# Set-up weights in later buffers; expert routing done by groups inside the layer loop, its last entries written at the start of the expert block

## The reference, cut to what matters

```python
logits = x_flat @ router_w.T
probs = jax.nn.softmax(logits, axis=-1)
top_v, top_i = jax.lax.top_k(probs, K)                  # K = 2
top_v = top_v / jnp.sum(top_v, axis=-1, keepdims=True)
for k in range(K):
    pos = (rank of the token among those whose k-th choice is this expert)
    keep = pos < C                                      # C = 1280
    h = jax.nn.gelu(jnp.einsum('ech,ehf->ecf', expert_in, w1), approximate=False)
    y = jnp.einsum('ecf,efh->ech', h, w2)
    out = out + tok * (gate * keep)[:, None]
```

## Time and profile before

| | us |
|---|---|
| median of 3 runs | 1517.16 (1514.6 to 1522.25) |
| the profiled execution, its own time | 1516.38 |
| its span, first to last instruction | 1514.6 |
| stack phase, last logits copied at | 932.1 |
| first products of an expert block at | 986.2 |
| last products end at | 1504.2 |

### The profile page before, as it was taken

How to read it: one execution, slowest core, us unless ns; L and a number is a source line. 1 busy time by engine, 2 the same in 40 slices (tenths; PEclk the granted TensorE clock), 3 DMA queues, 4 the chain that set the end, 5 groups by cost and what they waited for, 6 DMA issues and landing times. The chain is left out here.

```text
span 1514.6 us, 51179 instructions
## 1 busy us (share of the span) xinstructions
PE 1386.4 (92%) x19679; PEld 1179.2 (78%) x19680; DVE 852.4 (56%) x2933; ACT 829.0 (55%) x2393; POOL 626.2 (41%) x1265
## 2 busy tenths in 40 slices
PE   4879999999999999999999985299999999999997
PEld 3557777777777777777777763199999999999996
DVE  3578888888888888888888864811111111111110
ACT  0378898988888898988888871111111111111110
POOL 0132434343343424343343320046555555555554
PEclk6799999999999999999999996589999999999999
DMA  9423343434343433434342003446655665566653
GB/s 300 139 68 93 106 118 92 117 96 127 93 131 93 115 110 100 116 94 122 93 118 72 13 13 133 168 149 189 183 173 176 187 186 178 173 182 192 181 174 80
DMA packets 94784, 198.57 MB, mean 131 GB/s; under 512 B 14561, under 2 KB 49058, under 8 KB 84482
## 3 DMA queue, kind: packets, MB, share of 16 engines
q1 hardware_dynamic: 75698, 173.97, 37.1%
q0 software_dynamic: 15904, 18.66, 5.8%
q10 hardware_dynamic: 2992, 3.28, 0.6%
HBM read 177.88 MB, written 17.99 MB: 129 GB/s over the span
## 5 line engine op out<-in xcount | busy, mean ns | idle before, releaser
L1678 ACT ACTIVATE heT<-ps 128x512 f32<-128x512 f32 x142 | 84.8, 597 | 434.9 <-PE ps L1644 434.9
L1644 PEld LDWEIGHTS ps<-xeT,w_block 128*128 128x128 f32 x2272 | 267.5, 194 | 5.2 <-DVE xeT L1575 0.9
L1644 PE MATMUL ps<-xeT,w_block 128*128 128x128 f32 x2272 | 268.2, 277 | 1.0 <-DVE xeT L1555 0.5
L833 ACT ACTIVATE x_prob<-ps,x_nmax 128x257 f32<-128x257 f32 x512 | 237.4, 476 | 47.6 <-DVE x_rinv L1210 38.4
L1630 PE MATMUL ps<-w,heT 128*128 x1136 | 256.8, 379 | 0.0
L1630 PEld LDWEIGHTS ps<-w,heT 128*128 128x128 f32 x1136 | 210.5, 190 | 25.6
L1206 DVE TENSOR_REDUCE x_nmax<-ps 128x2 f32<-128x514 f32 x256 | 167.0, 684 | 19.9 <-PE ps L595 13.2
L1692 POOL TENSOR_TENSOR rt_hold<-constants 128x1 f32<-128x1 f32 x213 | 82.5, 387 | 219.3 <-DMA out<-ye,to_ix 134.0
L603 PE MATMUL ps<-constants,x_prob 128*128 128x128 f32 x1024 | 148.7, 277 | 20.4 <-ACT x_prob L833 19.8
L921 POOL TENSOR_TENSOR query_var_eps<-query_moments,epsilon 128x1 f32<-128x1 f32 x32 | 6.1, 190 | 370.3 <-DVE query_moments L1075 370.3
L837 ACT ACTIVATE x_probT<-ps 128x512 f32<-128x512 f32 x256 | 140.4, 600 | 25.3 <-PE ps L603 24.8
(11 more groups left out here) (283 smaller groups left out, 2841.0 us busy)
## 6 DMA issues: line engine op xcount, KB each, us to landing
w_block<-in_m_w SPq DMA_DIRECT2D x71, 1024.0 KB, 5.1
context<-in_cT SPq DMA_DIRECT2D x128, 257.0 KB, 3.1
context<-in_cn SPq DMA_DIRECT2D x128, 256.0 KB, 4.2
w<-in_m_w SPq DMA_DIRECT2D x8, 1024.0 KB, 12.0
xin<-in_x SPq DMA_DIRECT2D x32, 128.0 KB, 3.0
lastq<-in_lastq SPq DMA_DIRECT2D x32, 128.0 KB, 3.0
context<-in_lastk SPq DMA_DIRECT2D x32, 128.0 KB, 3.8
out<-x SPq DMA_DIRECT2D x32, 128.0 KB, 1.7
```

The source lines that it names most:

```text
L833: A(p1[u % 2][:, r, :], ps[:, r, 0:KEYS], ACT.Exp, bias=nmax1[u % 2][:, r:r + 1], accum_out=rsum1[u % 2][:, r:r + 1]).then_inc(e1_ok.handl ...
L1644: t = mm(ps[:, 2 * b + n, f * P:(f + 1) * P], w1[b][:, k, lo:lo + P], xeT[b][:, k, :], start=k == 0, stop=k == H - 1)
L1678: A(heT[b][:, n * FK // 2:(n + 1) * FK // 2, :].rearrange("p k t -> p (k t)"), ps[:, 2 * b + n, :], ACT.Gelu).then_inc(heT_ok.handle, 1)
```

## The change

**Set-up weights** move to buffers of the stack phase that are used later (`fw_raw` in the probabilities of the 16-head attention, `setup_w` in `query_blocks`, `x5`, `x5_norm`, `outT`). The waits of SP for the end of set-up are gone; each first context is loaded with 3 DMAs in place of 9, and x of tiles 1 to 3 comes right behind context 0.

**Experts' weights** `w2` now share the memory of the ring of contexts: two experts are loaded when one of the last four tiles is done with its context.

**Routing** is done by groups of four tiles in the loop (groups of two for the last four tiles). Per group DVE has 15 `CHOICE` instructions in one slot (the first and second expert, running counts) and 16 `PLACE` instructions in the next (gate, position, address), ACT one exponential, PE two small matmuls (`counted`). Each token's entry (its number and its gate) is written by an indirect DMA of POOL to a table in DRAM, 128 entries per DMA, two DMAs per tile. Tiles 0 to 27 are written in the loop and behind it; tiles 28 to 31 (8 DMAs) at the start of the expert phase. The table of blocks (`block_table`) is computed in between the last `PLACE` steps. Then SP loads the whole table into `places`; a block's rows are one column of it, whose number DVE loads into a register. The gather of gates is gone.

**The order** of the steps in `slot` is new on all engines, as are the banks `B`; s now ends at 35.

```diff
-AHEAD, BEHIND = 6, 3
+AHEAD, BEHIND = 6, 4
+GROUP = 4
+ROUTED_BEHIND = 3
...
-    fw_raw = [context[2][:, n * H * FF:(n + 1) * H * FF] for n in (0, 1)]
+    fw_raw = [p1_both[:].rearrange("p q r k -> p (q r k)")[:, 0:H * FF], p1T_both[:].rearrange("p q r k t -> p (q r k t)")]
...
             load_x(0, 0)
...
-            for b in range(NB):
-                load_batch(0, 0, b)
+            load_context(0, 0)
+            for t in range(1, RING):
+                load_x(t, t)
...
             for t in range(1, RING):
-                load_x(t, t)
-            for b in range(NB):
-                load_batch(1, 1, b)
-            sp.wait_ge(su_cp, SU_CP)
-            sp.wait_ge(su_q, SU_Q)
-            for t in range(2, RING):
-                for b in range(NB):
-                    load_batch(t, t, b)
+                load_context(t, t)
...
+            def write_entry(t, k):
...
+                nc.gpsimd.indirect_dma_start(table, bass.IndirectOffsetOnAxis(ap=place[:, t, k:k + 1], axis=0), entries[:, t, k, :], None).then_inc(table_in, 16)
...
+            CHOICE = [(route_best, route_shifted), (route_first_key, route_first_top), (route_first_hot, route_rest), (route_second, route_second_key),
+                      (route_second_rank, route_second_top), (route_second_hot, route_run(0)), (route_run(1), route_run(2)), (route_run(3),)]
+            PLACE = [(route_sum, route_share), (route_second_share,), (route_where, route_carry), (route_held, route_kept),
+                     (route_gate, route_both), (route_both_columns, route_address), (route_address_sum, route_whole), (route_column, route_column_f, route_place)]
...
+            last = len(GROUPS) - 1
+            for steps in CHOICE:
+                for step in steps:
+                    step(last, *GROUPS[last])
+            table_steps = block_table()
+            for steps in PLACE:
+                for step in steps:
+                    step(last, *GROUPS[last])
+                    next(table_steps, None)
...
+            for t in range(tiles - 4, tiles):
+                for k in range(TOPK):
+                    g.indirect_dma_start(table, bass.IndirectOffsetOnAxis(ap=place[:, t, k:k + 1], axis=0), entries[:, t, k, :], None).then_inc(table_in, 16)
...
+                if first:
+                    sp.wait_ge(table_in, TOPK * tiles * 16)
+                    sp.dma_start(places[:], table.rearrange("(p c) w -> p c w", c=ROW)[:, 0:EXP * tiles + 1, :]).then_inc(places_in, 16)
```

More of the change, by code:

```diff
@@ L124, with stack_phase @@
 RING = 4
-AHEAD, BEHIND = 6, 3
-def stack_phase(nc, t_in, const, logits, ps, constants, consts_loaded, zero, gates, xnorm, out, tiles, sem, sig, sb):
+CONTEXT = NB * KT * D + H * NB * KEYS + NB * OWN
+ROW = 512
+AHEAD, BEHIND = 6, 4
+GROUP = 4
+ROUTED_BEHIND = 3
+def stack_phase(nc, t_in, const, logits, ps, constants, consts_loaded, zero, contexts, w2, w2_in, table, table_in, tab_i, place, entries,
+                xnorm, out, tiles, cap, sem, sig, sb):
     ident = const["ident"]
@@ new lines, in stack_phase @@
+    blocks_i = sb("rt_blocks_i", [P, EXP], I32)
+    tab = sb("rt_tab", [P, 2])
+    GROUPS = [(t, GROUP) for t in range(0, tiles - GROUP, GROUP)] + [(tiles - 4, 2), (tiles - 2, 2)]
+    routed = Steps(sem("routing_step"), ["best", "shifted", "first_key", "first_top", "first_hot", "rest", "second", "second_key", "second_rank", "second_top", "second_hot",
+                                        "sum", "share", "second_share", "where", "held", "kept", "gate", "both", "both_columns", "address", "address_sum",
+                                        "whole", "column", "column_f", "place"])
@@ new lines, in stack_phase, with group_at, tiles_scattered @@
+    tab_ps, tab_ok = sem("block_table_in_psum"), sem("block_table_ready")
+    def group_at(s, half):
+        for g, (first, n) in enumerate(GROUPS[:-1]):
+            if first + n + ROUTED_BEHIND + half == s:
+                return g
+    def tiles_scattered(s):
+        for g, (first, n) in enumerate(GROUPS[:-2]):
+            done = first + n + ROUTED_BEHIND + 2
+            for i in range(n):
+                if s == done + (i if g < len(GROUPS) - 3 else i // 2):
+                    yield first + i
@@ new lines, in _, with routing @@
+            PLACE = [(route_sum, route_share), (route_second_share,), (route_where, route_carry), (route_held, route_kept),
+                     (route_gate, route_both), (route_both_columns, route_address), (route_address_sum, route_whole), (route_column, route_column_f, route_place)]
+            def routing(s, j):
+                for half, steps in enumerate((CHOICE, PLACE)):
+                    g = group_at(s, half)
+                    if g is not None:
+                        for step in steps[j]:
+                            step(g, *GROUPS[g])
@@ L1321, in _ @@
+                at(s + 4, c0_max)
+                at(s + 3, s0_scaled)
             for s in SLOTS:
                 slot(s)
-def expert_phase(nc, t_in, const, logits, ps, xnorm, gates, out, tiles, cap, blocks, sem, sig, sb):
+            last = len(GROUPS) - 1
+            for steps in CHOICE:
[6 more added lines that the diff above has]
+                    next(table_steps, None)
@@ L1331, in expert_phase @@
+            for _ in table_steps:
+                pass
+def expert_phase(nc, t_in, const, ps, xnorm, table, table_in, places, tab_i, place, entries, w2, w2_in, out, tiles, blocks, sem, sig, sb):
     ident = const["ident"]
-    T = tiles
-    tokens = tiles * P
-    GROUP, groups = 4, tiles // 4
     w1 = [sb(f"w1_block{b}", [P, H, FF]) for b in (0, 1)]
-    w2 = sb("w2", [P, EXP, FK, D])
     hold = sb("rt_hold", [P, 1])
-    prob = sb("rt_prob", [P, T, EXP])
-    prob2 = sb("rt_prob2", [P, T, EXP])
@@ L1362, in expert_phase @@
[L1362 to L1372 removed]
+    place_gate = places[:].bitcast(F32)
```

895 lines of the change are left out of this document (476 added, 419 removed), and 6 rows, old and new, of the table B.

## The result

The changed kernel takes 1511.15 us (median of 13 runs, 1507.46 to 1512.95) against 1520.17 us for the kernel before (13 runs, 1514.6 to 1523.38); the ratio is 0.9942, with a 95% interval from 0.9932 to 0.9952. That is 9 us less, just over the half per cent that can be told from no change. The forecast was 1493 and the range ended at 1507, so the sign was right and the size was not: 14 us of the forecast gain of 23 are missing.

A forecast was written before the change was run, and what follows sets the result against it. The prediction took PE to bound the loop and the experts, and a DVE chain the stretch between. Start -8.4, hand-over -20.5 and loop +5.5 summed to -23.4 us: 1516.4 to 1493 us, with an 8-in-10 range of 1476 to 1507.

The forecast's parts named there:

- Start: Set-up and first tiles: earlier lastq gives -7.1 us, earlier contexts 2 and 3 -1.3; together -8.4 us.
- Hand-over: From the last tile's norm to the first expert products: 20.5 us shorter, from 56.5 us before.
- (a) to (e): Hand-over from the last norm until POOL starts its last scatters: DVE steps, PE counts, table turn, crossing; sum 16.8 us.
- the crossing: Part of (e) in the hand-over: going over from one code block to the next, put at 0.7 us.
- Rival 4: Hand-over slower than the sum, scatters at 1.62 us and landing after 6 us: +7 us, 1500; 8%.
- Loop: Stack phase tiles: routing on DVE +6.5, PE's counts 2, new order and fewer bank waits -3; sum +5.5 us.
- Rival 1: Loop: DVE becomes the bound in slots with routing, no step hides, 42 us in place of 6.5: 1528; 6%.
- Rival 5: Loop: busy DVE holds up scatters, 1.62 us each; 24 tiles cost 30 us: 1523; 5%.
- Expert blocks: The 71 PE-bound blocks after the hand-over: products unchanged, register loads hidden; 0 us, at most +5.
- (d): Hand-over: 33 DVE steps, PLACE and block table in turns, as 17 pairs and four single steps; 4.4 us.
- (f): Hand-over: POOL issues 8 indirect DMAs at 0.99 us; last starts 7.2 us later, lands 3.5 us after its start.
- Rival 2: Loop: new order cuts PE's waits from 0.68 to 0.2 us a tile and DVE hides all routing: 1474; 14%.

The follow-up runs named there:

- e7: Changed kernel with both scatters of a slot moved into POOL's longest wait: 1501.06 us, ratio 0.9877 to the kernel before.
- e9: e7 with the bias of the self-attention's input moved behind the last key of unit 0 on POOL: ratio 0.9946 to the kernel before.
- e10: e7 with POOL building the query blocks later, behind the last key of unit 3: ratio 0.9925 to the kernel before.
- e12: e7 run a second time, on another chip: 1500.43 us, ratio 0.9885 to the kernel before.
- e1: Changed kernel with the 56 scatters of tiles 0 to 27 issued behind POOL's last slot instead of in the loop: 1557.6 us.
- e3: Changed kernel with x and lastq of tiles 1 to 3 loaded behind the small weights again: ratio 0.9984 to the kernel before.
- e6: Changed kernel with the four scatters of tiles 28 and 29 issued behind POOL's last slot, ahead of the expert block: ratio 0.9948 to the kernel before.
- e11: e7 with the bias of the self-attention's input moved ahead of the variance and rstd on POOL: ratio 0.9875 to the kernel before.
- e2: e1 with choice, counts and places of all groups also moved behind the last slot: 1573.3 us; tiles 17 to 21 take 104.31 us.

## Why the prediction was wrong, point by point

**Start: right in size, wrong in what became of it.** Undoing the two edits costs 6.4 and 3.0 us where I had 7.1 and 1.3. But start and drain together gained only 2.9 us, so some 6.5 us were lost again at the ends of the loop. A tile now takes 371.40 - 217.70 = 153.7 us from its first maximum to its norm in the steady loop, 141.15 before, since the last stages stand further behind; for the last tile it is 107.7 against 98.9. My sentence that the steps ahead of the last norm (2 us) and PE's better order (2 us) are equal was the step that failed here: the drain also holds two more groups' choice, and the old order's depth was taken for granted. Some 2 us of the loss belong to the places of the scatters: from tile 30's activation to the last norm it is 93.4 to 93.8 us in e7, e9, e10 and e12 and 92.5 in e1, but 95.9 in the changed kernel and 94.2 to 96.8 in e3 to e6, which have the scatters where it has them (e11 doesn't fit, at 95.6). What of the rest belongs to the depth and what to the routing steps in the drain was not separated.

**Hand-over: right.** 18.3 of 20.5 us. DVE's steps and PE's counts, terms (a) to (e) without the crossing, took 961.81 - 945.25 = 16.6 us (16.1 forecast). The crossing took 2.5 instead of 0.7: the scatters of tiles 24 to 27 were to end some 6 us ahead of it, but they ended at 958.73, 3.1 us before DVE's last step, and POOL entered 5.62 us behind them. The eight scatters took 8.8 instead of 7.2 between first and last start, since 0.3 us lie between two; SP asked for the table 2.1 us after the last one's start, 3.5 forecast. Rival 4 had the place right and the cause wrong: no scatter took 1.62 us, and they landed 2.2 us after their start (median).

**Loop: the step that failed.** Forecast +5.5 us, measured +18.5 in 26 tiles. In the terms of the sum:
- new order and fewer waits for banks: the tiles ahead of the first group, at 104.15 / 4 = 26.04 us, make 677.0 for 679.4, so -2.4 (-3 forecast). With e2's 104.31 us it is 678.0 and -1.4, and the next term is 12.3.
- routing: 690.3 - 677.0 = +13.3 for 11 slots of routing in this stretch, 1.2 us a slot with PE's counts in it. I had 0.5 us and 0.3 a group, 7.0 for the same stretch. The trace says where it is lost: in four tiles PE waits 0.9 us for `x` and 0.6 for `ffn_xq`, which stand in DVE's queue behind steps of `CHOICE` and `PLACE`, and its four small products take about 0.5 (an estimate from their starts, 324.64 to 325.03). That is 2.0 of the 2.44 us of a group; the rest is not accounted for. The mechanism was that of Rival 1, at half of the 2.3 us from which it decides. A routing step isn't always 0.2 us either: `rt_shifted` took 0.52 beside an addition of POOL and `rt_column` 0.70, for 0.17 and 0.16 in the hand-over.
- scatters: 697.9 - 690.3 = +7.6, forecast 0. This is the term that I put at nothing. I had the 11.6 us that POOL waited in one piece before and called the scatters hidden "where they don't stand ahead of something due". The order listing showed that they do, and I priced only the case in which they themselves are slow (Rival 5). They are not: 1.05 us in the loop, 0.96 behind it. Nor is the 11.6 us wait there in the new order, where POOL's longest is 4.0. What they put off on POOL then hit a DVE instruction.

The Trainium skill, SBUF — State Buffer, section "SBUF: two separate sides", says that the port pair of DVE and GpSimd is an exclusive lock, held for the whole instruction, so that the one that comes second stands still. The rows agree: a norm of 0.41 us lasts until 0.15 us after POOL's addition, wherever that one ends (0.80, 0.97), and POOL's 0.72 us become 1.17 where DVE came first. I had cited the section for the scatters' descriptors alone. The 3100 ns that I took from the section "A bandwidth-pool intuition that's wrong" are not seen in this case: the longest scatter in the loop took POOL 1.18 us, and from issue to landing it was 2.3 us in the loop and 2.2 behind it (medians).

**Expert blocks: 0 forecast, 2.6 us less.** From the first block's products to the second's it is 989.56 - 983.45 = 6.1 us, at a granted clock of 0.73, and was 993.58 - 986.15 = 7.4 at 0.59: 1.3 us. The clock had been at 0.50 before in both kernels (975 to 986 and 965 to 983). The other 1.3 lie behind the last products (9.1 us to the end, 10.4 before). Why the clock rose sooner was not tried.

**Sums that don't come out.** In (d), 17 pairs and four single steps are 38 steps, not 33; the 33 took 3.9 us (956.30 to 960.23) for my 4.4, and the bound with each at 0.2 is +2.2, not +3.0. In (f), 7 starts of 0.99 us are 6.9, not 7.2. Rival 2 adds up to 1472, not 1474. DVE's free time was 26.1 - 22.3 = 3.8 us a tile, and the 1.9 were only the two waits shown, so that 24.7 us of work would still have left 1.4 free. None of these moves the forecast by more than 0.5 us.

**The best version** is e7 (e11 is equal to it): 1501 us, 0.9877 of the kernel before and, by the two ratios, 0.65% under the changed kernel, by moving two lines.

## What to carry to other kernels

An operation on an idle engine is hidden only if nothing behind it in that engine's queue is due: put it in the engine's longest wait, by name, and here eight scatters in four tiles cost nothing where they had cost 1.9 us. When an order changes on DVE or POOL, compare the mean time of each DVE group at the same count before and after; a norm that goes from 0.41 to 0.80 us tells of a neighbour on POOL, and such a move has to be read from the trace again, since three of four made the slots longer and the fourth changed the whole time by less than can be measured. Small steps spread over an engine that is busy for 85 to 89% of the bound's time are not nearly hidden: a slot's routing added 2.1 us to DVE's busy time (97.2 - 92.9 in two slots) and 1.2 us to the loop, where I had put 0.5. Look for what PE waits for behind them in the queue, and price that.

## What the runs showed of the hardware

- A DVE instruction of the kinds `TENSOR_SCALAR` and `TENSOR_TENSOR` that starts beside an elementwise instruction of POOL gets longer: 0.35 to 1.16, 0.41 to 0.80 or 0.97, 0.74 to 1.26, 0.69 to 1.10, 0.17 to 0.52 us. In all of these it ends as if it had begun 0.1 to 0.3 us before the POOL instruction's end, so that a short one ends just behind it and one of 0.7 us 0.56 us behind it. POOL's additions and powers lengthen beside DVE too, 0.72 to 1.17 and 0.55 to 1.01. `TENSOR_REDUCE` from PSUM kept its 0.68.
- A scatter by POOL of 8 bytes a row takes 0.96 us with DVE nearly idle and 1.05 in the loop, and 0.30 us lie between two in a row.
- With indirect DMAs issued ahead of a block's end, POOL entered the next block no sooner than 5.62 us after the last of them in any kernel here (5.62 in six, 5.95 in e6), and where that was over earlier (e7 and e9 to e12), 1.2 us after DVE's last step. What takes these 5.6 us was not tried.
